# Third phase of a decoder kernel: head norms of the first sequences begun ahead of the first maximum, second group's steps one slot towards the front

## What is computed

```python
x = x + _L1_attn_ref(_layernorm(x), ...)      # the change is here
x = x + _L1_xattn_ref(_layernorm(x), ctx, ctx, ...)
x = x + _L1_ffn_ref(_layernorm(x), ...)

# _L1_attn_ref: 16 heads of 8 channels
q = (x @ Wq.T).reshape(N, L, H, D).transpose(0, 2, 1, 3)     # k, v likewise
q = _layernorm(q, gq, bq)                                    # over the 8 channels of a head
k = _layernorm(k, gk, bk)
scores = where(causal, einsum('nhld,nhmd->nhlm', q, k), NEG)
out = einsum('nhlm,nhmd->nhld', softmax(scores), v)
return out @ Wo.T + bo
```

## Time and profile before

| | |
|---|---|
| median of 3 runs | 1635.24 us (1632.71 to 1641.94) |
| the profiled execution | 1637.81 us, span 1636.1 us |
| TensorE busy | 1425.1 us (87%) |
| VectorE busy | 1210.3 us (74%) |
| ScalarE busy | 1123.4 us (69%) |
| GpSimd busy | 578.7 us (35%) |
| third phase | from about 1053 us to the end |

### The profile page before, as it was taken

One profiled execution on the slowest core, in us unless ns is written; L12 is line 12 of the kernel. 1 busy time (PEld: TensorE's weight loads), 2 busy tenths in 40 slices (PEclk: granted clock), 3 DMA queues, 4 the chain that ended last, 5 costly groups with the idle time before them and its releaser, 6 DMA issues. The chain is left out here.

```text
span 1636.1 us, 42886 instructions
## 1 busy us (share of the span) xinstructions
PE 1425.1 (87%) x15385; PEld 1058.7 (65%) x15385; DVE 1210.3 (74%) x2848; ACT 1123.4 (69%) x2842; POOL 578.7 (35%) x623
## 2 busy tenths in 40 slices
PE   2358999999999999999974999777899999999995
PEld 0125777777777767677763888645667677776663
DVE  3999789898988887765545555467678898887665
ACT  1127998888888888798852556445667767767652
POOL 0011424343524343314014100155446656444452
PEclk9999999999999999999995999869999999999997
DMA  6733231423232121100121222230000110000000
GB/s 173 163 94 77 52 85 47 106 51 87 58 79 69 49 73 46 66 21 13 61 65 50 61 58 61 59 83 18 8 23 10 37 36 10 22 21 2 22 9 14
DMA packets 78012, 87.56 MB, mean 54 GB/s; under 512 B 11120, under 2 KB 67312, under 8 KB 73328
## 3 DMA queue, kind: packets, MB, share of 16 engines
q1 hardware_dynamic: 70192, 72.58, 17.6%
q0 software_dynamic: 4096, 8.40, 1.8%
q10 hardware_dynamic: 3520, 3.84, 0.7%
HBM read 66.97 MB, written 17.83 MB: 52 GB/s over the span
## 5 line engine op out<-in xcount | busy, mean ns | idle before, releaser
L893 ACT ACTIVATE pr<-P,nm 128x256 f32<-128x256 f32 x512 | 237.8, 490 | 4.1 <-DVE nm L1043 4.0
L1943 ACT ACTIVATE et<-P 128x1024 f32<-128x1024 f32 x128 | 131.3, 1026 | 106.0 <-PE P L1730 105.6
L1043 DVE TENSOR_REDUCE nm<-P 128x4 f32<-128x1024 f32 x128 | 156.5, 1222 | 59.2 <-PE P L694 53.6
L324 POOL TENSOR_TENSOR rstd<-ve,mhalf 128x1 f32<-128x1 f32 (+2 forms) x83 | 76.9, 928 | 245.9 <-DVE ve L319 245.0
L877 ACT COPY ptS<-P 128x512 f32<-128x512 f32 x256 | 136.8, 585 | 32.9 <-PE P L708 28.2
L708 PE MATMUL P<-ident,pr 128*128 128x128 f32 x1024 | 140.1, 280 | 9.5 <-issue 7.2
L868 ACT ACTIVATE pr<-pr,ri 128x256 f32<-128x256 f32 x256 | 118.8, 522 | 33.9 <-DVE pr L1034 33.2
L692 PE MATMUL P<-kt_w,qt_b 64*128 64x128 f32 x1024 | 127.1, 309 | 3.2 <-ACT pr L893 2.7
L708 PEld LDWEIGHTS P<-ident,pr 128*128 128x128 f32 x1024 | 110.3, 142 | 26.2 <-issue 13.8
L2103 DVE TENSOR_REDUCE qS<-P 128x8 f32<-128x1024 f32 x64 | 78.4, 1226 | 56.4 <-PE P L1723 55.4
L607 POOL TENSOR_TENSOR kv_w<-kv_w,r_w1h 128x512 f32<-128x512 f32 x48 | 61.1, 1273 | 164.2 <-DVE pr L1034 164.2
(11 more groups left out here) (325 smaller groups left out, 4138.8 us busy)
## 6 DMA issues: line engine op xcount, KB each, us to landing
kv_w<-scr_v SPq DMA_DIRECT2D x16, 1024.0 KB, 8.0
r_w1h<-scr_r SPq DMA_DIRECT2D x16, 1024.0 KB, 10.8
xt<-scr_xs SPq DMA_DIRECT2D x71, 64.0 KB, 1.8
scr_ys<-yt SPq DMA_DIRECT2D x71, 64.0 KB, 1.5
x<-in_x SPq DMA_DIRECT2D x8, 256.0 KB, 9.4
scr_v<-mixing SPq DMA_DIRECT2D x8, 256.0 KB, 2.0
scr_r<-mixing SPq DMA_DIRECT2D x8, 256.0 KB, 2.1
xb<-in_x SPq DMA_DIRECT2D x8, 256.0 KB, 4.5
```

The source lines that it names most:

```text
L324: nc.gpsimd.tensor_tensor(rstd[:, k, lo:hi], ve[:, k, lo:hi], mhalf[:, lo:hi], ALU.pow).then_inc(S[rs_sem], 1)
L893: e = nc.scalar.activation(pr[:, s % 3, h * KEYS:(h + 1) * KEYS], scores(s)[:, h // 2, (h % 2) * KEYS:(h % 2 + 1) * KEYS], ACT.Exp, bias=n ...
L1043: nc.vector.tensor_reduce(nm[:, s % 3, 0:4].rearrange("p (a h) -> p a h", a=2), scores(s).rearrange("p a (h k) -> p a h k", k=KEYS), AX.X, ...
L1943: nc.scalar.activation(et[:, u % 4, :, :, :], scoresT, ACT.Exp).then_inc(S["h_exp"], 1)
```

## The change

Three things are changed, all of them places in the order of work; one step is written out in a second place, and nothing is added to the work or taken from it.

- Head norms of sequence 1: reduction, guess and first step from slot -3 to -5, the rest from -2 to -3. Of sequences 2 and 3: reduction and guess from slot 0 to -1 (slot 0's maximum stands first in slot 0), the three steps, keys and queries all in slot 0, where the last step, keys and queries were in slot 1.
- Second group: scaling from slot 2 to 1, transposition from 3 to 2, projections from 4 and 5 to 3 and 4, head norms from 4 to 6 to 3 to 5, `kt0` and `qt0` from 7 to 6, `kt1` from 8 to 7. `qt1` and the rest stay.
- The second group's shift was at the beginning of slot 2, ahead of the statistics in VectorE's order; it now stands behind the statistics at the end of slot 1, under the name `nm_late`.

```diff
--- before.py
+++ after.py
@@ -86,7 +86,7 @@
         "sum0": -40, "sum1": -38, "sum2": -30, "sum3": -29, "stat0": -28, "stat1": -27, "nm": -26, "xn0": -26, "xn1": -26,
         "dxt": -25, "bias": -25, "qk0": -24, "qk1": -23, "qk2": -22, "qk3": -21, "square": -21, "v": -19, "reduce": -20,
         "guess": -18, "inv0": -18, "inv1": -16, "inv2": -15, "kn": -14, "qn": -13,
-        "qp": None, "kt0": -13, "qt0": -12, "kt1": -11, "kt2": -7, "qt2": -6, "qt1": -5, "kt3": -2, "qt3": -1}
+        "qp": None, "nm_late": None, "kt0": -13, "qt0": -12, "kt1": -11, "kt2": -7, "qt2": -6, "qt1": -5, "kt3": -2, "qt3": -1}
 SELF_BY_SLOT = {
     0: {**{name: None for name in ("stat0", "stat1", "nm", "xn0", "xn1", "dxt", "qk0", "qk1", "qk2", "qk3", "square", "v",
                                    "reduce", "guess", "inv0", "inv1", "inv2", "kn", "qn", "qt0", "qt1", "qt2", "qt3")},
@@ -94,10 +94,10 @@
         "sum0": -12, "sum1": -11, "sum2": -10, "sum3": -6, "bias": 4,
         "kt0": -5, "kt1": 0, "kt2": 1, "kt3": 2},
     1: {"load": -43, **{f"gather{k}": at for k, at in enumerate((-9, -9, -5, -5, -4, -4, -3, -3))},
-        "sum0": -1, "sum1": 0, "sum2": 1, "sum3": 1, "stat0": 1, "stat1": 1, "nm": 2, "xn0": 2, "xn1": 2,
-        "dxt": 3, "bias": 7, "qk0": None, "qk1": None, "qk2": None, "qk3": None, "qp": 4, "square": 4, "v": 5,
-        "reduce": 5, "guess": 5, "inv0": 5, "inv1": 6, "inv2": 6, "kn": 6, "qn": 6,
-        "kt0": 7, "qt0": 7, "kt1": 8, "qt1": 8, "kt2": 9, "qt2": 11, "kt3": 12, "qt3": 13},
+        "sum0": -1, "sum1": 0, "sum2": 1, "sum3": 1, "stat0": 1, "stat1": 1, "nm": None, "nm_late": 1, "xn0": 1, "xn1": 1,
+        "dxt": 2, "bias": 7, "qk0": None, "qk1": None, "qk2": None, "qk3": None, "qp": 3, "square": 3, "v": 4,
+        "reduce": 4, "guess": 4, "inv0": 4, "inv1": 5, "inv2": 5, "kn": 5, "qn": 5,
+        "kt0": 6, "qt0": 6, "kt1": 7, "qt1": 8, "kt2": 9, "qt2": 11, "kt3": 12, "qt3": 13},
     2: {**{f"gather{k}": 1 + k // 2 for k in range(2 * GS)},
         "sum0": 4, "sum1": 5, "sum2": 6, "sum3": 7, "stat0": 7, "stat1": 7, "nm": 8, "xn0": 8, "xn1": 9,
         "dxt": 10, "bias": 10, "qk0": 11, "qk1": 12, "qk2": 13, "qk3": 14, "square": 14, "v": 12, "reduce": 15,
@@ -109,8 +109,8 @@
 FRONT = {"pow": (-12, -11, -10, -6), "nm": (-11, -10, -8, -4), "dx": (-10, -9, -7, -3), "qkv": (-9, -8, -6, -2)}
 PARTS = ((0, 1), (1, 2), (2, 4))
 PART_AT = ({"square": -9, "reduce": -9, "guess": -9, "inv0": -8, "inv1": -7, "inv2": -7, "kn": -7, "qn": -7},
-           {"square": -8, "reduce": -3, "guess": -3, "inv0": -3, "inv1": -2, "inv2": -2, "kn": -2, "qn": -2},
-           {"square": -2, "reduce": 0, "guess": 0, "inv0": 0, "inv1": 0, "inv2": 1, "kn": 1, "qn": 1})
+           {"square": -8, "reduce": -5, "guess": -5, "inv0": -5, "inv1": -3, "inv2": -3, "kn": -3, "qn": -3},
+           {"square": -2, "reduce": -1, "guess": -1, "inv0": 0, "inv1": 0, "inv2": 0, "kn": 0, "qn": 0})
 
 
 LOCAL = {"load": -10, "e_stat0": -8, "e_stat1": -4, "e_stat2": -2, "e_stat3": 0, "e_nm0": -7, "e_nm1": -3, "e_nm2": -1,
@@ -2205,6 +2205,9 @@
                             ln_heads(dve, 0, [2 * k, 2 * k + 1], home(g), "d_mv")
                             if k:
                                 ln_eps(dve, 0, 0, GS, "d_mv", GS * g + GS, "d_ve")
+                    g = self_at(s, "nm_late")
+                    if g is not None:
+                        ln_shift(dve, 0, 0, GS, "d_rs", norms(g), "d_nm")
 
 
                     for k in range(4):
```

## The result

Over 20 executions of each kernel the changed one takes 1639.49 us (median) and the one before 1635.55, a ratio of 1.0021 with a 95% interval of 1.0014 to 1.0028: **3.4 us slower** (2.3 to 4.6, by the ratio; the medians differ by 3.9), where 2.5 us faster was forecast. It is inside the 0.5% within which I had put 0.89, and on the other side. The profiled execution of the changed kernel took 1637.08 us, span 1635.4, so it is one of its quicker ones, the second of 20.

A forecast was written before the change was run, and what follows sets the result against it. TensorE was taken to bound the phase's body, so only the front counted: slot 9 2.9 us early, less 0.1 for the first query copy and 0.3 for clock, gives 2.5 us, from 1635.24 to 1632.7 us; range 1627.5 to 1638.5.

The forecast's parts named there:

- What bounds the kernel: Third phase: TensorE bounds the body, so the change only shifts it, by where slot 9 opens; later work is the same.
- Second part: Head norms moved to slots -5 and -3: they fit a VectorE idle stretch, first query copy about 0.1 us late.
- Third part: Head norms moved to slots -1 and 0: keys ready before the second maximum, so slot 2 opens 2.0 us earlier.
- the hole: Slot 1: TensorE idles 1.91 us waiting for sequence 2's keys; the change was to close this.
- Second group's first steps: Slots 1 and 2: TensorE newly waits for the scaled group, so slot 3 opens 1.9 us late.
- Projections: Slots 3 and 4: slot 4 opens 2.5 to 3.5 us late, slot 5 0.3 to 1.4 late.
- Norms of the second group: Slots 4 and 5: VectorE needs 3.7 us, or 5.3 if it meets GpSimd's selection; slot 6 opens 1.9 late.
- Slots 7 and 8: With one transposition each they take 4.5 us, so slot 9 opens 2.9 us early.
- The clock: TensorE's clock falls in the front can't be told: -1.0 to +3.6 us, taken as +0.3.
- The first: Rival: new wait in slot 2 and low clock through slots 3 to 5 win, slot 9 1.5 to 2 us late; 0.20.
- The third: Rival: early norms only move the wait from keys to the scaled group; within 1 us of nothing; 0.15.
- the warning about gathers: Norms beside gathers: VectorE's two-port operations keep GpSimd from writing DMA descriptors; a gather 0.2 us late would change nothing.

The follow-up runs named there:

- parts_only: Kernel before with only the first group's head norms at their new places, second group as before; ratio 0.9981 to before, 3.1 us faster.
- after_bias3: Changed kernel with GpSimd's bias of the first group in slot 3 instead of 4; ratio 1.0007 to the kernel before.
- xn_dxt_only: Kernel before with only the second group's shift, scaling and transposition one slot earlier; ratio 1.0009 to before.
- after_kt3_early: Changed kernel with sequence 3's keys and queries of the first group transposed in slot 1, not 2; ratio 0.9993 to the kernel before.
- after_again: Changed kernel, unchanged, run and traced a second time; ratio 1.0017 to the kernel before.

## Why the prediction was wrong

Two terms of the sum failed most. The second group's norms were priced at one hold of VectorE by a selection (1.6 us), and took one of 3.04 us and a second one. And the sum ended at slot 9, as if nothing could differ behind it, while slot 10 took 7.1 us for 3.7 in the changed kernel.

**What bounds the kernel** was right: from slot 12 to slot 127 both kernels run parallel within 0.2 us in each trace. "Slots 9 onward carry the same work in both kernels" was wrong. TensorE's work is the same there, but it waited in slot 10 (3.4 us more than before) once slots 7 and 8 got shorter.

**Second part** was right: the copy after it comes at 11.40 us of the phase (1070.41), before at 11.47, so it costs nothing.

**Third part** was right in kind, a gain in slot 2 of 1.5 for 2.0 us; by itself it carries through to the end as 3 us (parts_only). That is more than the hole's 1.9 us: in the trace of parts_only slot 2 gives 0.9 back, and slots 4 and 7 are shorter by 1.6 and 1.1 us. Slot 4 was so in the second trace of before too (from +0.8 to -0.9), by the clock, so that part of the trace's 3 us is luck; for slot 7 I had no term.

**Second group's first steps.** The new wait was the right mechanism and in its place. Its size was short by 1.2 us: slot 3 opens 3.1 late, not 1.9. Of that, 0.4 were missing as the copy ended: the scaling was 0.6 late, because the second maximum was. For the other 0.8, I had taken the transpositions behind it at full clock (0.9 to 1.1); TensorE had idled for 2.3 us in slot 2 and did the keys at 1.11, as slot 1 did in the earlier trace rows, and the queries and the mask at 1.06.

**Projections** fitted: slot 4 +3.2 for +2.5 to +3.5, slot 5 +0.2 for +0.3 to +1.4.

**Norms of the second group: the first step whose error lasted** (slot 5 had still opened at +0.2, for +0.3 to +1.4). I priced a meeting with one selection (1.6 us). In slot 4 GpSimd's bias of the first group stands right behind the selection, and VectorE is held from the end of a gather through both: 3.04 us. The table said "bias": 4, and I had not laid the moved steps beside it. after_bias3 shows that this is what held VectorE. Then slot 6 didn't take 6.05 but 7.7 us: it opened after an idle 3.36 us at the lower clock (a mask at 1.03) and VectorE met a second hold, 1.74 us for an operation of 0.29 (L356 at 1110.23). Slots 7 and 8, at 3.6 and 4.6 for 4.5 each, gave back more than I had thought, so that slot 9 opened at -0.6, 2.3 us from the forecast.

**The step that isn't in the prediction at all** is slot 10, 3.4 us longer in the first trace and 3.9 in the second, and it is the largest. In the first trace the sum is: 2.3 us short at slot 9, 0.9 won back in slot 9, 3.4 lost in slot 10, 0.3 won back in slot 11, together the 4.5 between -2.9 and +1.6. From slot 12 on it is the forecast's rigid shift. Of the second group's moved steps I had counted each instruction and each engine's wait, but not that shorter slots bring GpSimd's run of three gathers (3.5 us, from 1126.63 to 1130.15; the 3.85 in my expectation is 0.3 too long) and its selections late.

**The clock** I called unknown, with -1.0 to +3.6 us; the two traces of the changed kernel differ by 2.6 us in slot 3 for it alone. By the rule of the Trainium skill ("TensorE: Matmul & The Clock Gate", section "What's actually happening") that activity releases the throttle, the rise would have come earlier. These traces don't bear it out: slot 2's scores came 1.5 us earlier and began at the lower level, and the granted clock rose 29.0 us into the phase (at 1088.0), against 28.5 before and 28.3 in the second trace of the changed kernel.

**Rivals.** The first, 1.5 to 2 us slower, had the right side. Its mechanism is half of the cause: the wait in slot 2 with the low clock behind it is shown by xn_dxt_only, after_kt3_early and after_again; the other half, the stall of slot 10, belonged to no rival. I gave it 0.20, as I thought its price had to be paid on top of a gain of 2.9 us that was 2.3 too large. The third, that the early norms only move the wait to the scaled group, describes slot 2 as the traces show it (-1.5 and +3.1, without the norms -0.2 and +2.9), but not the time, since slot 10 came on top.

**A thin reading.** The gather of the earlier trace rows ran beside the first maximum and a reduction, not beside the other operations of the norms, so that row couldn't speak on the warning about gathers. Nothing hung on it in the sum, and the gathers of the traces shown here take 0.95 to 0.99 us.

**Open** are the path by which GpSimd's gathers hold ScalarE's scaled queries in slot 9, and what makes slot 1 open 1.1 to 1.4 us late in eleven of the thirteen traces, one of the two of the kernel before among them; no run took these apart.

## What to carry to other kernels

A moved step has to be laid beside every engine's table of that slot, not only beside the waits it has itself: here three gathers that nobody moved made one slot 3.4 us longer, more than the whole forecast gain. When slots in the middle of a software pipeline get shorter, list the engine that has the longest fixed run in them (here GpSimd, 3.5 us of gathers and 2.15 of selections), since it becomes the next bound for that slot even at 35% busy. And split such a change into its halves before judging it, and don't expect the halves to add up: one alone gained 3 us, the other alone lost 3, and together they lost 3.4. Three entries of a table turned that into a gain of 4.9, of which the first half alone has 3.1.

## What the hardware showed that I had not expected

An operation of VectorE on 128x128 elements that takes 0.27 us can last until GpSimd's work is over, from the end of a gather through two operations on end: 3.04 us in the changed kernel, in both its traces and in those of four variants 3.04 to 3.05. With one selection behind the gather a like operation lasted 1.60.

The same kernel ran most of slot 3 at 2.4 GHz in one execution and all of it at 1.2 in another, a difference of 2.6 us that stays to the end. Single traces of such a front aren't to be compared without a second one.
